# One order for all engines laid over the whole run: image embedding first, two banks and fifty steps rearranged, block closed without GpSimd's drain

## The reference, cut to what matters

```python
tokens = einsum('bpi,hi->bph', patches, W) + b            # embedding, times pos_embed
h = concatenate([cls * pos, tokens * pos, txt], axis=1)
# A: retention with complex weights, per head of 16, 8 heads
xn = layernorm(h); q, k, v = xn @ wq, xn @ wk, xn @ wv     # complex
y = real((q @ k.T * decay_mask) @ v); yn = norm_per_head(y) * gn_scale + gn_bias
h = h + (silu(real(xn @ w1)) * yn) @ real(w2)
# B: softmax attention, C: layernorm, router, one expert of eight per token
x2 = layernorm(h); o = softmax(q @ k.T / 4) @ v @ Wo + bo
t = layernorm(x2 + o) * ln1_g + ln1_b
e = argmax(t @ gate_W + gate_b); gw = max(softmax(...))
out = h + gw * (gelu(t @ W1[e] + b1[e]) @ W2[e] + b2[e])
```

## Time and profile before

| | us |
|---|---|
| median of 3 runs | 1430.12 |
| lowest, highest | 1424.32, 1433.03 |
| profiled execution | 1419.48 |
| its span, first to last instruction | 1417.7 |
| PE, DVE, ACT, POOL busy | 1348.5, 1010.9, 722.7, 408.4 |
| granted clock, mean of the span | 0.977 |

### The profile page before, as it was taken

One profiled execution on the slowest core, in us unless ns is written; L12 is line 12 of the kernel. 1 busy time (PEld: TensorE's weight loads), 2 busy tenths in 40 slices (PEclk: granted clock), 3 DMA queues, 4 the chain that ended last, 5 costly groups with the idle time before them and its releaser, 6 DMA issues.

```text
span 1417.7 us, 40337 instructions
## 1 busy us (share of the span) xinstructions
PE 1348.5 (95%) x14878; PEld 989.9 (70%) x14879; DVE 1010.9 (71%) x2331; ACT 722.7 (51%) x1630; POOL 408.4 (29%) x268
## 2 busy tenths in 40 slices
PE   6889999999999999999999999999999775999996
PEld 5556666666666666666666666666666444999996
DVE  1477777777777777777777777777778853766664
ACT  2145555555555555555555555555555543556553
POOL 0000222222222222222222222222222233656664
PEclk9999999999999999999999999999999975999999
DMA  8522332232223322323232222222320011343331
GB/s 292 215 83 72 83 84 83 84 83 83 84 84 83 84 84 84 83 83 84 83 84 83 84 84 84 83 84 83 84 83 14 14 30 37 105 125 103 103 101 48
DMA packets 94842, 124.61 MB, mean 88 GB/s; under 512 B 56587, under 2 KB 77117, under 8 KB 94176
## 3 DMA queue, kind: packets, MB, share of 16 engines
q1 hardware_dynamic: 38112, 102.47, 23.1%
q0 software_dynamic: 56576, 19.93, 6.5%
HBM read 101.27 MB, written 20.82 MB: 86 GB/s over the span
## 4 chain that ended last, share of the span: by engine, by line
PE 90%; DVE 4%; DMA 2%; issue 2%; ACT 1%; POOL 0%; SPq 0%; POOLq 0%; DVEq 0%; ACTq 0%
PE bank_emb L421 20%; PE bank_s L475 9%; PE bank_z L411 7%; PE bank_y L489 7%; PE bank_x L411 7%; PE bank_s L710 6%; PE bank_s L553 4%; PE bank_s L541 4%; PE bank_s L411 3%; PE bank_y L411 3%; PE bank_y L581 3%; PE bank_x L699 3%; PE bank_y L699 3%; PE bank_x L563 3%; PE bank_s L525 2%; PE bank_y L553 2%
## 5 line engine op out<-in xcount | busy, mean ns | idle before, releaser
L1397 POOL DMA_INDIRECT expert_rows<-row_sb,placei x128 | 275.7, 2154 | 627.7 <-DVE z L1058 575.6
L421 PE MATMUL bank_emb<-home_x 128*128 128x256 f32 (+1 forms) x1216 | 324.0, 393 | 3.5 <-DMA home_x<-in_x_main 2.5
L421 PEld LDWEIGHTS bank_emb<-home_x 128*128 128x128 f32 (+1 forms) x1216 | 221.4, 192 | 103.4 <-issue 47.4
L998 DVE TENSOR_TENSOR home_s<-bank_s,con 97x776 f32<-97x776 f32 x256 | 239.8, 958 | 25.9 <-PE bank_s L475 13.8
L1012 DVE TENSOR_REDUCE mx<-bank_s 97x8 f32<-97x776 f32 x128 | 120.3, 960 | 57.9 <-PE bank_s L541 57.8
L1409 POOL DMA_INDIRECT out_tokens<-yo,tok x104 | 123.1, 1184 | 73.6 <-issue 52.5
L475 PE MATMUL bank_s<-qm,xn 32*97 32x452 f32 x1024 | 132.6, 580 | 4.2 <-DVE home_s L1017 2.0
L1017 DVE TENSOR_TENSOR home_s<-bank_s,mx 97x776 f32<-97x776 f32 x128 | 120.6, 963 | 3.3
L853 ACT ACTIVATE home_s<-home_s 97x776 f32<-97x776 f32 x128 | 108.4, 847 | 26.4 <-DVE home_s L1017 26.4
L710 PE MATMUL bank_s<-w2e,home_s 128*128 x832 | 110.6, 276 | 0.0
L1005 DVE COPY vp<-bank_s 97x128 f32<-97x128 f32 x256 | 70.1, 285 | 54.9 <-PE bank_s L475 54.8
(11 more groups left out here) (206 smaller groups left out, 2339.8 us busy)
## 6 DMA issues: line engine op xcount, KB each, us to landing
home_x<-in_x_main SPq DMA_DIRECT2D x96, 768.0 KB, 7.2
home_x<-expert_rows SPq DMA_DIRECT2D x104, 129.0 KB
w1e<-in_exp_w SPq DMA_DIRECT2D x1, 2576.0 KB, 10.8
txt<-in_txt_t SPq DMA_DIRECT2D x32, 64.0 KB, 2.3
w2e<-in_exp_w SPq DMA_DIRECT2D x1, 2048.0 KB, 16.1
expert_rows<-row_sb,placei POOLq DMA_INDIRECT x128, 8.1
out_tokens<-yo,tok POOLq DMA_INDIRECT x104
home_x<-in_x_tail SPq DMA_DIRECT2D x32, 48.0 KB, 2.6
```

The lines of the kernel that those rows point to most:

```text
L421: mm = pe.matmul(banks["emb"][:, 0:NPG], wtok[0:k, c, :], x_sb[0:k, c, :], start=(c == 0), stop=(c == KC - 1))
L998: ins = dve.tensor_tensor(sm[:, k % 2, 2 * h:2 * h + 2, :], pair(h), decay, ALU.mult)
L1397: pool.indirect_dma_start(out=rows[:, :], out_offset=bass.IndirectOffsetOnAxis(ap=placei[:, k, c:c + 1], axis=0), in_=row_sb[:, k, c, E:E ...
```

## The change

It replaces the lists of steps on PE, ACT and DVE and the table `USES` by others; changes the start: weights of the embedding in four pieces, each ahead of its piece of x, constants behind them on three semaphores, the embedding of group 0 ahead of the products of weights, `woc` copied first; moves the write of the blank rows behind the expert weights; and closes the block with `no_gpsimd_drain=True`. A round now has the distances `b_wo` i - 2, `a_gate` i - 1, `a_var` i, `place_index` i - 3, `b_probs_t(0, 2)` i - 1. No computation is added or left out.

```diff
 USES = [
-    ("B.wo", "z", 3), ("B.scores1.0", "s0 s1", 2), ("B.scores1.1", "s2 s3", 2), ("C.var2", "z", 3), ("A.qr", "z", 0),
...
+    ("B.scores1.0", "s0 s1", 2), ("B.scores1.1", "s2 s3", 2), ("A.var", "z", 0), ("C.var2", "z", 3),
+    ("A.gate", "z", 1), ("A.scores3.0", "s0 s1", 1), ("A.scores3.1", "s2 s3", 1), ("A.qr", "x", 0), ("A.qi", "s1", 0),
...
-EXP_ORDER = [(1, 1, 2), (1, 0, 2), (0, 0, 2), (0, 1, 1)]
-MAX_ORDER = [(1, 1, 2), (1, 0, 2), (0, 1, 1), (0, 0, 1)]
+EXP_ORDER = [(0, 0, 2), (1, 0, 2), (1, 1, 2), (0, 1, 1)]
+MAX_ORDER = [(1, 0, 2), (1, 1, 2), (0, 0, 1), (0, 1, 1)]
...
-        block = ctx.enter_context(nc.Block())
+        block = ctx.enter_context(nc.Block(no_gpsimd_drain=True))
...
-            sp.dma_start(con[:], consts).then_inc(s_c, 16)
-            sp.dma_start(wts[:], weights).then_inc(s_c, 16)
-            sp.dma_start(col[:], columns).then_inc(s_c, 16)
-            sp.dma_start(pos[:], pos_t).then_inc(s_c, 16)
-            sp.dma_start(tokno[:], token_no).then_inc(s_c, 16)
-            sp.dma_start(wtok[:, 0:KC - 1, :], w_main).then_inc(s_w, 16)
-            sp.dma_start(wtok[0:KTAIL, KC - 1, :], w_tail).then_inc(s_w, 16)
...
             for k in range(4):
+                if k < 3:
+                    sp.dma_start(wtok[:, XP[k]:XP[k + 1], :], w_main[:, XP[k]:XP[k + 1], :]).then_inc(s_w[k], 16)
+                else:
+                    sp.dma_start(wtok[0:KTAIL, KC - 1, :], w_tail).then_inc(s_w[k], 16)
                 load_x(0, k)
+            sp.dma_start(col[:], columns).then_inc(s_c, 16)
+            sp.dma_start(pos[:], pos_t).then_inc(s_c, 16)
+            sp.dma_start(wts[:], weights).then_inc(s_k, 16)
+            sp.dma_start(con[:], consts).then_inc(s_k, 16)
...
-            pe.wait_ge(s_c, 80)
+            def ahead(g, c0, c1):
+                if g:
+                    embed(g, c0, c1)
+
+            embed(0, 0, KC)
+            pe.wait_ge(s_k, 32)
             pe.wait_ge(s_neg, 1)
...
             pe.wait_ge(s_made, 1)
+            pe.wait_ge(s_c, 32)
...
             for i in range(FIRST, LAST):
-                at(b_wo, i - 3)
-                at(embed, i + 1, 4, 5)
+                at(ahead, i + 1, 2, 3)
                 at(b_scores, i - 2, 1)
-                at(embed, i + 1, 5, 9)
+                at(ahead, i + 1, 3, 4)
+                at(a_var, i)
+                at(ahead, i + 1, 4, 6)
                 at(c_var, i - 3)
...
             act.wait_ge(s_mm, 1)
+            act.copy(woc[:], banks["s2"][:, 0:P]).then_inc(s_made, 1)
             act.copy(ar[:], banks["s0"][:, 0:P])
...
-            act.copy(woc[:], banks["s2"][:, 0:P]).then_inc(s_made, 1)
...
+            tokens(0)
+            dve.wait_ge(s_k, 32)
+            dve.tensor_copy(run[:], const("run0")).then_inc(s_zero, 1)
+            dve.wait_ge(s_zero, 1)
+            dve.wait_ge(s_made, 2)
...
             def a_residual(g):
                 ps = full(dve, g, "A.out")
+                if g:
+                    full(dve, g - 1, "B.hrows")
...
+                at(tokens_ahead, i + 1)
+                at(b_max, i - 1, 0, 0)
+                at(b_max, i - 1, 0, 1)
+                at(b_shift, i - 1, 0, 0)
+                at(b_shift, i - 1, 0, 1)
+                at(b_divide, i - 2)
                 at(a_value_rows, i, 2, 1)
-                at(a_value_rows, i, 2, 0)
-                at(a_decayed, i, 2, 0, last=True)
+                at(a_decayed, i, 2, 0)
+                at(a_value_rows, i, 2, 0, last=True)
                 at(a_decayed, i, 2, 1, last=True)
-                at(place_sum, i - 3)
-                at(gate_one, i)
```

More of the change, by code:

```diff
@@ L259, in fusion @@
         s_xused = [sem(f"x_used{k}") for k in range(4)]
-        s_w, s_c, s_txt, s_blankin = sem("wtok_loaded"), sem("constants_loaded"), sem("txt_loaded"), sem("blank_loaded")
+        s_w = [sem(f"wtok_loaded{k}") for k in range(4)]
+        s_c, s_k, s_n = sem("columns_loaded"), sem("constants_loaded"), sem("token_numbers_loaded")
+        s_txt, s_blankin = sem("txt_loaded"), sem("blank_loaded")
         s_neg, s_mm, s_made, s_zero = sem("neg_wqi_ready"), sem("weight_products"), sem("weights_made"), sem("vector_set_up")
@@ L344, in _ @@
             load_txt(0)
+            sp.dma_start(tokno[:], token_no).then_inc(s_n, 16)
             sp.dma_start(blank[:], no_token).then_inc(s_blankin, 16)
-            sp.wait_ge(s_blankin, 16)
-            sp.dma_start(rows[E * REG:E * REG + P, :], blank[:]).then_inc(s_blankin, 16)
             def load_group(i):
@@ L358, in _ @@
             sp.dma_start(w2e[:], exp_w2).then_inc(s_ew, 16)
+            sp.wait_ge(s_blankin, 16)
+            sp.dma_start(rows[E * REG:E * REG + P, :], blank[:]).then_inc(s_blankin, 16)
             with sp.Fori(2, NG) as i:
@@ L462, in a_gate, with a_scores @@
                 product(g, "A.gate", weight("w1"), xn[:, g % 2, :])
-            def a_scores(g, k):
-                if k == 0:
+            def a_scores(g, k, first=False):
+                if first:
                     read(pe, g, "A.qr")
@@ L527, in b_values, with b_scores @@
                 done(mm, "B.v")
-            def b_scores(g, k):
-                if k == 0:
+            def b_scores(g, k, first=False):
+                if first:
                     read(pe, g, "B.q")
@@ L658, in _ @@
                 at(a_scores, i, 1)
+                at(b_center, i - 1)
                 at(b_probs_t, i - 2, 1, 0)
-                at(b_center, i - 1)
-                at(embed, i + 1, 18, 19)
-                at(b_probs_t, i - 2, 0, 2)
                 at(b_probs_t, i - 2, 0, 1)
                 at(b_var, i - 1)
-                at(b_probs_t, i - 2, 1, 1)
+                at(ahead, i + 1, 16, 18)
+                at(b_values, i - 2)
                 at(b_probs_t, i - 2, 0, 0)
-                at(b_probs_t, i - 2, 1, 3)
-                at(embed, i + 2, 0, 1)
-                at(b_values, i - 2)
+                at(c_rank, i - 3)
                 at(b_k, i - 1)
                 at(b_q, i - 1)
-                at(a_center, i + 1)
-                at(embed, i + 2, 1, 2)
-                at(b_scores, i - 1, 0)
-                at(b_mix, i - 2, 0)
+                at(b_probs_t, i - 2, 0, 3)
+                at(b_probs_t, i - 2, 1, 3)
+                at(ahead, i + 1, 18, 19)
+                at(b_scores, i - 1, 0, first=True)
                 at(b_sums, i - 2, 0)
                 at(b_sums, i - 2, 1)
-                at(b_mix, i - 2, 1)
-                at(a_var, i + 1)
-                at(c_rank, i - 3)
-                at(embed, i + 2, 2, 4)
-                at(a_scores, i, 2)
                 at(a_mix, i, 0)
                 at(a_mix, i, 1)
-                at(a_gate, i)
+                at(b_mix, i - 2, 0)
+                at(b_mix, i - 2, 1)
+                at(a_scores, i, 2)
+                at(b_wo, i - 2)
+                at(b_probs_t, i - 1, 0, 2)
+                at(ahead, i + 2, 0, 2)
+                at(a_center, i + 1)
                 if i == LISTED:
@@ L890, in _ @@
             for i in range(FIRST, LAST):
+                at(a_square, i)
+                at(b_exp, i - 2, 0, 0)
+                at(c_square, i - 3)
+                at(a_log, i)
+                at(c_log, i - 3)
+                at(a_rstd, i)
+                at(gate_exp, i - 1)
+                at(c_rstd, i - 3)
                 at(gate_log, i - 1)
                 at(gate_sigmoid, i - 1)
-                at(c_square, i - 3)
-                at(c_log, i - 3)
+                at(b_exp, i - 2, 1, 0)
@@ L895, in _ @@
+                at(a_query, i, 1)
+                at(a_query, i, 0, last=True)
+                at(y_square, i - 1)
                 at(b_exp, i - 2, 1, 1)
-                at(a_query, i, 0)
-                at(a_query, i, 1, last=True)
-                at(c_rstd, i - 3)
-                at(b_probs_copy, i - 2, 0, 3)
-                at(y_square, i - 1)
                 at(y_log, i - 1)
                 at(y_rstd, i - 1)
-                at(b_exp, i - 2, 1, 0)
+                at(b_row_copy, i - 2)
```

110 lines of the change are left out of this document (55 added, 55 removed), and 17 rows, old and new, of the table USES.

## The result

The changed kernel takes **1407.10 us** (median of 4 runs, 1403.12 to 1409.17), the kernel before 1429.55 beside it (4 runs, 1424.32 to 1433.03): a ratio of 0.9843, 95% interval [0.9805, 0.988], 22.5 us less. The forecast was 1404, 26 less. The total is near, but two terms of the sum are far off, in opposite directions. The profiled execution of after took 1403.12 us, its span is 1401.3 (before 1419.48 and 1417.7).

A forecast was written before the change was run, and what follows sets the result against it. The prediction took TensorE's matmuls in their order to bound the middle rounds, with other losses at the ends. Drain -7.2, start and filling -9, rounds -6 and emptying -4 gave -26 from 1430: 1404 us, range 1390 to 1419.

The forecast's parts named there:

- what makes the others longer stays: Assumption moving the sum from the profiled 1419.5 us to the median 1430.1, which lies 10.6 higher.
- End of the block: Block end: without GpSimd's drain the span ends about 0.2 us after SP, 7.2 us less.
- Its rival: Block end: GpSimd's drain covers something waited for anyway, so -19 in all, 1411 us; chance 0.18.
- Start and filling: Start until 100 us: earlier embedding, a_var(0) 8.0 us sooner, less waiting for x; 9 us less.
- One round: Middle rounds: fewer narrow-mode changes less losses at tight joints, 0.2 us a round, 6 us less over 29 rounds.
- the prediction's own sign: Stated test: forecast wrong if the start gives less than 5 us or a round gets longer.
- The three joints: Within a round, C.var2, the gate and b_var have no room; 0.2 us of loss taken.
- fewer ways into narrow modes: TensorE's round: 5 ways into narrow matmul modes instead of 7, at 0.20 us each, 0.40 us less a round.
- Emptying: Pipeline's end: shorter path from B's scores to C's rows and b_wo moved, 4 us less, bounds 1 and 8.
- the round isn't PE's: Rival: something other than PE paces the round, only the ends count, -20, 1410 us; chance 0.10.
- All goes well: Rival: no loss at the joints (-12 instead of -6), one half-clock stretch less (-4 more), 1394 us; chance 0.17.
- Joints that feed each other: Slower rival: VectorE runs late, shifting wo, residual and next scores round after round, 1448 us; chance 0.05.

The follow-up runs named there:

- F: Set of follow-up kernels sharing one letter and one chip; the kernel before took 1421.0 us beside them.
- G: Set of follow-up kernels sharing one letter; on its shared chip the kernel before took 1420.3 us.
- E3: The kernel before with one edit, the block closed without GpSimd's drain: 1423.1 us against 1430.2, ratio 0.9942.
- G0: The changed kernel itself, run again on another chip beside the kernel before (1420.3 us): 1385.9 us, ratio 0.9761.
- E4: The changed kernel with the kernel before's engine orders and bank table, keeping the new start and no GpSimd drain: 1415.3 us, ratio 0.9905.
- G2: Same program as E4, the changed kernel with the old orders, run again beside the kernel before (1420.3 us): 1405.8 us, ratio 0.9899.
- E1: The changed kernel with two embedding pieces of group i+2 moved between A's and B's mixes: 1450.1 us, ratio 1.0144.
- F1: The changed kernel with the place index moved behind B's division, so GpSimd's scatters start about 6.5 us later: 1410.9 us, ratio 0.9925.
- F3: The changed kernel with the edits of E1 and F1 together: 1443.5 us, ratio 1.0163.

## Why the prediction was right in sum, step by step

**Which before.** The sum was made against a profiled execution of 1419.5 us and moved to the median of 1430.1 on the assumption that "what makes the others longer stays". Now the 10.6 us have a name. The profiled execution is of the kind of F and G (no group with a scatter held up, the kernel before at 1419 to 1421); E3 shows the old order on the other kind, 0.33 us a round more, and its 28 rounds take 982.6 us where those of the profiled execution take 974.1: 8.5 of the 10.6. After was profiled on that other kind, so 34.79 against 35.55 us a round compares two kinds of chip. By the mean of 16 rounds the fair pairs are 35.12 and 35.55 there (E3, after), 34.81 and 34.84 here (before, G0).

**End of the block, -7.2.** Right. SyncE's drain is at 1401.0 in after and the last instruction at 1401.3; E3 gives 7.1 by itself. Its rival (the drain covers something waited for anyway) is refuted.

**Start and filling, -9.** Right: a_var(0) at 23.31 and not 30.36, -7.0 (forecast -8.0, since the constants landed at 17.6 and not at 16.8); a_var(3) -9.9 against before. E4 beside E3 gives 7.8 for the whole.

```profile
6.26 10.85 PE L427 MATMUL bank_emb<-home_x 128*128 128x256 f32 x38 [6.26 <-DMA home_x<-in_x_main]
18.09 0.46 PE L441 MATMUL bank_s<-wts 128*128 128x128 f32 x2 [0.99 <-ACT neg_wqi L762]
...
23.31 0.92 PE L415 MATMUL bank_z<-sqa,con 128*128 128x388 f32 x2
```

**One round, -0.2 us and -6 in all.** This is the step that failed, also by the prediction's own sign, "the forecast is wrong if [...] a round gets longer": it got longer, from 35.12 to 35.55 us on the kind of chip of the result, and on the other it did not get shorter by the mean. Where nothing holds the mixes up, 15 of G0's 27 rounds from a_var(3) on last 34.70 to 34.73 us, against 34.79 in most rounds of before: -0.08. The three joints that the prediction named cost what it said, seen in the starts of after:

```profile
639.38 0.89 PE L415 MATMUL bank_z<-sqc,con 128*128 128x388 f32 x2
640.10 1.03 PE L427 MATMUL bank_emb<-home_x 128*128 128x256 f32 x4
641.03 0.89 PE L415 MATMUL bank_z<-xn,wts 128*128 128x388 f32 x2
641.85 0.64 PE L486 MATMUL bank_s<-qm,xn 32*97 32x452 f32 x4
```

C.var2 takes 0.72 where it took 0.65, the gate 0.82 where it took 0.76, b_var, by the starts in both traces, 0.76 where it took 0.68: 0.21 together, forecast 0.2, too small for the list of waits. So the fewer ways into narrow modes gave some 0.3 by subtraction, not 0.40. What is left, 0.08 or 2 us in all, the holes of the long narrow run eat in the other 12 rounds (last section), so G0's 28 rounds take 0.7 us more than before's. And on the chip that the result comes from, the new order put two scatters into that run instead of one beside A's second mixes, so each round loses 0.7 there and not 0.33. The prediction looked for waits on VectorE and ScalarE; GpSimd's scatters it never placed against PE's row, although the two orders give the place and the profile the length. But no row of before could have shown the price, since in that trace a scatter starts 0.10 us ahead of A's mixes and costs nothing.

**Emptying, -4.** Wrong by far in size. What the step reckoned came: B's scores of the last group to C's rows take 5.6 us (1165.93 to 1171.52), forecast 5.8, before 8.4. But it took only that chain. The matmuls between a_var(3) and a_var(31) are equally many, so the two ends can be added, whatever work changed sides (99 matmuls did). G2 and G0, one chip: 105.7 + 119.8 = 225.5 us with the old order, 104.3 + 98.5 = 202.8 with the new, **-22.7**. Of it PE idle is 50.4 less 36.3, so 14.1, and PE busy 175.2 less 166.5, so 8.6, at a granted clock in the emptying of 0.83 where it was 0.75: with fewer gaps less of the work ran at the lower level of 1.2 GHz. That the new order fits the partial rounds of both ends better is my reading; no run changed one end alone. The waits show it at four places, which are 8.8 of the 14.1, G2 first, then G0, where the two for home_s are not in the list (it has others for home_s, 1.2, 1.0 and 0.8):

```profile
PE bank_x L619 <- DVE th L1088: 5.5, 2, 2.8
PE bank_x L627 <- DVE onehot L1127: 3.4, 1, 3.4
PE bank_s L564 <- DVE home_s L1036: 2.6, 1, 2.6
...
PE bank_s L415 <- DVE home_s L1036: 2.2, 1, 2.2
```

```profile
PE bank_s L619 <- DVE th L1094: 2.7, 2, 2.3
PE bank_s L627 <- DVE onehot L1133: 2.2, 1, 2.2
```

**The rivals.** That the round isn't PE's: the mode changes and joints moved its length by their own amounts, so no, though its 1410 lay near the time measured. All goes well: the ends went better than that, the rounds worse. Joints that feed each other with VectorE late: 35.55 us a round was its sign, but no wait for VectorE stands in after's rounds.

**The sum.** For the fair pair on the chip of G: end and start -14.6 (G2 against the kernel before), order -19.9, in all -34.4 where -26 was said. On the chip of the result the hold-ups beside scatters take back about 12 of it, (35.55 - 35.12) x 28, and 22.5 are left. The forecast of 1404 was met because two errors, some 19 us of gain not seen at the ends and some 19 of rounds (6 not gained, 1 of holes, 12 of hold-ups), nearly cancel. That is luck: on the chip of G the same sum misses by 8 us.

## What to carry to other kernels

Profile both kernels beside each other on one chip before a per-round difference is explained, and compare a kernel with itself there. When an order is rebuilt, add up both partial ends by matmul count, not by the one chain that is easy to follow; they were worth 23 us here, four times the 6 us forecast for the full rounds. Place every scatter of GpSimd (2.15 us each, four in a row) against the other engines' rows like any other instruction: beside an SBUF-to-SBUF step of VectorE it made 0.36 us into 1.66, and on one kind of chip TensorE's narrow runs are longer beside it.

## What the hardware showed that I had not expected

- **One program, measured twice, 20 us apart.** The changed kernel takes 1407.1 and 1385.9, the kernel before 1429.6 and 1420.3; E4 and G2, one program on two chips, 1415.3 and 1405.8. The difference of the changed kernel lies in groups of column-narrow matmuls beside a scatter: 0.33 us where one scatter starts 0.10 ahead of 64 mixes (E3, E4), 0.85 where two start within a run of 160 (5.00 in after, 4.15 undisturbed in G0). Where it comes, PE goes on 1.2 to 1.3 us behind the scatter's start. What it is in the chip stays open, and so is whether moving the scatters there gives the time back.
- **A hold-up can hide behind the starts.** In E1 the starts are evenly spaced and the semaphore comes 1.36 us late; in after the starts have a hole of 0.6 and the semaphore of B's mixes is on time.
- **A long narrow run seems to outrun its instructions.** In traces without the hold-up, B's mixes still stop now and then: G0 8 times for 0.21 to 0.72 us, F1 6 times, before twice. Each time PE starts again 2.2 to 2.9 us behind the start of a packet on the instruction queue (115 packets of 16 KB for PE's nearly 30,000 instructions, so one in 12 us), 1.3 to 1.6 behind its end. With the run cut into 112 and 72 matmuls (F3, beside F1 on one chip) it did not happen once. The Trainium skill (Runtime: NRT & Kernel Launch, Instruction fetch mechanics) says that fetching is hidden since dispatch is slower than the fetch; with a matmul and its weight load every 0.023 us this trace differs.
- **A small step can take a scatter's length:** 1.66 us for 0.36 (F1, F3), in every round in which it started beside one.
